# Context attention: transposes moved from TensorE to transposing DMA transfers, products of probabilities and values placed behind both projections of a round

## The reference, cut to what matters

```python
D_MODEL, H, KVH, HD, EPS = 512, 16, 4, 128, 1e-6
q = x @ Wq.T                          # 128 x 2048
k, v = cat(ctx, x) @ Wk.T, cat(ctx, x) @ Wv.T   # 256 x 512
q, k = rope(rms_norm(q)), rope(rms_norm(k))
p = softmax(q @ k.T / sqrt(HD))       # per head 128 x 256
x = layernorm(x + (p @ v) @ Wo.T)
```

## Time and profile before

| | us |
|---|---|
| median of 3 runs | 3000.09 (2999.1 to 3002.46) |
| profiled execution: its own time | 3004.53 |
| its span | 3002.7 |
| TensorE busy | 2727.9 (91%) |
| VectorE busy | 1958.4 (65%) |
| ScalarE busy | 1574.4 (52%) |
| GpSimd busy | 1204.2 (40%) |
| mean granted TensorE clock | 0.969 |

### The profile page before, as it was taken

How to read it: one execution, slowest core, us unless ns; L and a number is a source line. 1 busy time by engine, 2 the same in 40 slices (tenths; PEclk the granted TensorE clock), 3 DMA queues, 4 the chain that set the end, 5 groups by cost and what they waited for, 6 DMA issues and landing times. The chain is left out here.

```text
span 3002.7 us, 49266 instructions
## 1 busy us (share of the span) xinstructions
PE 2727.9 (91%) x17011; PEld 1595.3 (53%) x17276; DVE 1958.4 (65%) x3681; ACT 1574.4 (52%) x3629; POOL 1204.2 (40%) x1238
## 2 busy tenths in 40 slices
PE   6789896899999999959976998998889999999998
PEld 4677672555555555524434665666654444444443
DVE  5778896878787888767656788887463232322335
ACT  7999983655555555464417777676432221222121
POOL 3889885745454545224333111111142212222121
PEclk8999997999999999989997999999989999999999
DMA  4111103100000000040012000000021111111211
GB/s 161 40 54 48 43 33 120 43 5 8 4 7 4 7 4 4 1 168 1 1 50 74 19 19 18 14 16 19 12 90 65 45 50 63 63 63 32 65 32 67
DMA packets 50541, 122.53 MB, mean 41 GB/s; under 512 B 7042, under 2 KB 11522, under 8 KB 48163
## 3 DMA queue, kind: packets, MB, share of 16 engines
q1 hardware_dynamic: 50338, 120.00, 12.3%
HBM read 111.25 MB, written 4.52 MB: 39 GB/s over the span
## 5 line engine op out<-in xcount | busy, mean ns | idle before, releaser
L2060 POOL TENSOR_TENSOR s_state<-s_state,s_ct 128x512 f32<-128x512 f32 x256 | 326.8, 1302 | 82.0 <-DVE s_state L2235 79.6
L2235 DVE TENSOR_TENSOR_SCAN s_state<-s_decay,s_psd 128x512 f32<-128x512 f32 x256 | 301.8, 1208 | 68.3 <-PE s_psd L2380 34.7
L1044 DVE TENSOR_TENSOR m_prod<-m_bank,m_gated 128x512 f32<-128x512 f32 x88 | 60.8, 691 | 437.6 <-ACT m_gated L853 437.6
L779 POOL TENSOR_TENSOR m_aTl<-m_prod,m_aTh 128x512 bf16<-128x512 f32 x88 | 101.8, 1157 | 584.0 <-ACT m_aTh L855 584.0
L853 ACT ACTIVATE m_gated<-m_bank 128x512 f32<-128x512 f32 x88 | 52.5, 597 | 437.3 <-PE m_bank L1166 437.3
L1156 PE MATMUL m_bank<-m_xTl,m_wh 128*128 128x512 bf16 x704 | 267.8, 380 | 3.1 <-ACT m_wh L819 1.0
L1155 PE MATMUL m_bank<-m_xTh,m_wh 128*128 128x512 bf16 x671 | 255.5, 381 | 2.4 <-DVE m_prod L1044 2.4
L2380 PE MATMUL s_psd<-ident,s_v 128*128 128x128 f32 x1024 | 166.0, 287 | 41.8 <-DVE s_state L2235 21.1
L2136 ACT ACTIVATE s_decay<-s_dt,s_nega 128x508 f32<-128x508 f32 x256 | 181.6, 710 | 20.4 <-DVE s_state L2235 20.3
L2149 ACT ACTIVATE s_v<-s_uT,s_bT 128x512 f32<-128x512 f32 x256 | 182.1, 712 | 0.8 <-PE s_psd L2380 0.7
L2380 PEld LDWEIGHTS s_psd<-ident,s_v 128*128 128x128 f32 x1024 | 123.1, 147 | 88.6 <-ACT s_v L2149 47.1
(11 more groups left out here) (516 smaller groups left out, 8070.2 us busy)
## 6 DMA issues: line engine op xcount, KB each, us to landing
s_ct<-ssm_bc SPq DMA_DIRECT2D x64, 256.0 KB, 3.2
m_scale<-moe_scale SPq DMA_DIRECT2D x64, 256.0 KB, 3.2
m_stage<-in_moe_w_dram SPq DMA_DIRECT2D x16, 768.0 KB, 5.0
m_stage<-in_moe_w_dram SPq DMA_DIRECT2D x8, 864.0 KB, 7.8
X<-in_x_dram SPq DMA_DIRECT2D x4, 1024.0 KB, 12.2
a_cf<-in_ctxT_dram SPq DMA_DIRECT2D x16, 256.0 KB, 2.7
a_wstage<-in_xa_wq_dram SPq DMA_DIRECT2D x8, 512.0 KB, 3.6
a_wstage<-in_xa_wo_dram SPq DMA_DIRECT2D x8, 512.0 KB, 4.0
```

Source lines behind the costliest of these rows:

```text
L2060: pool.tensor_tensor(h, h, ct[t % 4][:, s * P:(s + 1) * P].unsqueeze(1).broadcast_to([P, KB, P]), ALU.mult).then_inc(weighted, 1)
L2235: dve.tensor_tensor_scan(state[i % RING][:, :], decay[t % 2][:, s, :, :].rearrange("p m t -> p (m t)"), ps_d[i % 2][:, :], 0.0, ALU.mult, ...
```

## The change: what it does, and its diff

The transposes of `rot` and of the probabilities leave TensorE. What is to be turned is first split in high and low part in SBUF (`rotp`, `pp`), and SyncE issues transposing DMA transfers, each of 128 partitions x 1024 bf16 values (eight blocks of 128 x 128, 256 KB): one for each chunk 0 to 5 (both parts in it), two for each round's probabilities (high, low). That is 14 transfers a turn. `ps_t` goes, and its two banks make `ps_p` four buffers deep. ScalarE's `prob_high` now scales and rounds in one instruction per head (L1588), VectorE's `prob_low` scales and subtracts in one per head (L1705), in the same round as the exponentials; `normalize` shrinks to the reciprocal (`totals`). `turned_high` reads SBUF, and `turned_low` moves to GpSimd. Products of probabilities and values (`values`, `attn_high`, `attn_low`) stand behind the second chunk. SyncE's program is written out turn by turn, with the last five `wo` loads between the transfers of turn 0. The LayerNorm's `r` shares memory with a weight staging buffer.

```diff
@@ SyncE
+            def turn_chunks(n, g, j):
+                if g == 0:
+                    return
+                for c in (2 * g - 2, 2 * g - 1):
+                    r = c % 2
+                    sp.wait_ge(t_low.sem, t_low.at(n, c + 1))
...
+                    sp.dma_start(out, rotp[r][:, :, :].rearrange("p a n -> p (a n)"), transpose=True).then_inc(t_done[r].sem, 16)
+
+            def turn_probs(s, g):
+                for a, ready, done in ((0, p_high, ph_done), (1, p_low, pl_done)):
+                    sp.wait_ge(ready.sem, ready.at(s, g + 1))
+                    if a == 0 and (g or late(s, 1)):
+                        sp.wait_ge(pv.sem, pv.at(s, g) if g else pv.at(s - 1))
+                    sp.dma_start(pT[:, a, :, :, :].rearrange("p k h q -> p (k h) q"),
+                                 pp[:, a, :, :, :].rearrange("p k h t -> p (k h t)"), transpose=True).then_inc(done.sem, 16)
+
+            def turn(s, p, start=None, last=False, last_x=False):
+                for g in range(4):
+                    if g == 0 and not last_x:
+                        context(s + 2)
+                    if not last:
+                        turn_chunks(s + 1, g, 1 - p)
+                    if start == 0 and g:
+                        wl.sync(sp, wlow, first_wo + 2 * g + 1, min(first_wo + 2 * g + 3, nchunks))
+                    turn_probs(s, g)
@@ GpSimd
+            def turned_low(n, c):
+                pool.wait_ge(t_high.sem, t_high.at(n, c + 1))
+                pool.tensor_tensor(rotp[c % 2][:, 1, :], rot[c % 2][:, :], rotp[c % 2][:, 0, :], ALU.subtract).then_inc(t_low.sem, 1)
...
+                    if g and not last:
+                        turned_low(s + 1, 2 * g - 2)
                     if not last_x:
...
+                    if g and not last:
+                        turned_low(s + 1, 2 * g - 1)
                     if not last:
                         front(s + 1, g, 1 - p)
@@ ScalarE
             def exponentials(s, g, p):
                 act.wait_ge(shifted.sem, shifted.at(s, g + 1))
                 if g or late(s, 1):
-                    act.wait_ge(p_turned.sem, p_turned.at(s, 2 * g) if g else p_turned.at(s - 1))
+                    act.wait_ge(p_low.sem, p_low.at(s, g) if g else p_low.at(s - 1))
...
+                for h in range(GH):
+                    e = act.activation(pp[:, 0, :, h, :], prob[:, h, :].rearrange("p (k t) -> p k t", k=2), ACT.Copy, scale=rtotal[:, h:h + 1])
@@ VectorE
                 if c >= 2 or late(n, 1):
-                    dve.wait_ge(turned.sem, turned.at(n, c - 1) if c >= 2 else turned.at(n - 1, 5 + c))
+                    dve.wait_ge(t_low.sem, t_low.at(n, c - 1) if c >= 2 else t_low.at(n - 1, 5 + c))
...
-                for h in range(GH):
-                    m = dve.tensor_scalar(prob[:, h, :], prob[:, h, :], rtotal[:, h:h + 1], None, ALU.mult)
...
+                for h in range(GH):
+                    m = dve.scalar_tensor_tensor(pp[:, 1, :, h, :], prob[:, h, :].rearrange("p (k t) -> p k t", k=2), rtotal[:, h:h + 1], pp[:, 0, :, h, :],
+                                                 ALU.mult, ALU.subtract)
@@ TensorE, a round
                     scores(s, g, p)
-                    if g:
-                        turn_probs(s, g - 1, t_low.at(s) if g == 1 or last else t_low.at(s + 1, 2 * g - 2))
...
                     if not last:
                         chunk(s + 1, 2 * g, 1 - p)
+                    if g == 0 and not last_x:
+                        turn_x(s + 2, p)
+                    if not last:
+                        chunk(s + 1, 2 * g + 1, 1 - p)
                     if g:
                         values(s, g - 1, p)
                     elif start != 0:
                         values(s - 1, 3, 1 - p)
-                    if g == 0 and not last_x:
-                        turn_x(s + 2, p)
-                    if not last:
-                        turn_chunks(s + 1, g, 1 - p)
-                        chunk(s + 1, 2 * g + 1, 1 - p)
```

More of the change, by code:

```diff
@@ L1252, in stage_xattn @@
         woh, wol = (fr.sb(f"a_wo{n}", [P, 16, D], BF16, st) for n in "hl")
-        ln = LayerNorm(fr, st, "a")
+        wstage = [fr.sb(f"a_wstage{j}", [P, 1024], F32, st)[:, :] for j in range(3)]
+        ln = LayerNorm(fr, st, "a", r=wstage[2][:, 0:D])
         xs = fr.sb("a_xs", [P, D], F32, st)
@@ L1330, in stage_xattn @@
         v_low = Count(fr, "a_vlow", 2)
-        turned = Count(fr, "a_turned", 6)
+        t_done = [Count(fr, f"a_tdone{r}", 48) for r in range(2)]
         t_high = Count(fr, "a_thigh", 6)
@@ L1376, in _ @@
             wl.sync(sp, wlow, 4, first_wo)
[L1377 to L1380, removed]
+            turn_chunks(0, 1, 0)
+            wl.sync(sp, wlow, first_wo, first_wo + 3)
+            turn_chunks(0, 2, 0)
+            turn_chunks(0, 3, 0)
+            turn(0, 0, start=0)
+            for s in range(1, SEQS - 2):
+                turn(s, s % 2)
+            turn(SEQS - 2, 0, last_x=True)
+            turn(SEQS - 1, 1, last=True, last_x=True)
         @block.gpsimd
@@ L1469, in _ @@
             c_low_part(1, 1)
-            for g in range(3):
+            for g in range(4):
+                if g:
+                    turned_low(0, 2 * g - 2)
+                    turned_low(0, 2 * g - 1)
                 if g == 1:
@@ L1551, in turn @@
                         chunk(s + 1, 2 * g, 1 - p)
+                    prob_high(s, g)
+                    if g and not last:
+                        turned_high(s + 1, 2 * g - 1)
+                    if g == 0 and not last_x:
+                        x_high_part(s + 2, p)
+                    if not last:
+                        chunk(s + 1, 2 * g + 1, 1 - p)
                     if g:
@@ L1693, in turn @@
                         chunk(s + 1, 2 * g, 1 - p)
+                    prob_low(s, g)
+                    if g == 2 and not last_x:
+                        bound(s + 2)
+                    if not last:
+                        chunk(s + 1, 2 * g + 1, 1 - p)
                     if g:
@@ L1697, in turn @@
                         attn_low(s - 1, 3)
-                    if not last:
-                        turned_low(s + 1, g, 1 - p)
-                    if g == 2 and not last_x:
-                        bound(s + 2)
-                    if not last:
-                        chunk(s + 1, 2 * g + 1, 1 - p)
                     if g == 1 and start is None:
@@ L1811, in values @@
                     cols = slice(g * HD, (g + 1) * HD)
[L1812 removed]
+                    mm = three(pe, ps_v[:, :], (vh[p][:, k, cols], vl[p][:, k, cols]), [pT[:, a, k, :, :].rearrange("p h q -> p (h q)") for a in range(2)], k == 0, k == 1)
                 mm.then_inc(pv.sem, 1)
@@ L1825, in turn @@
                     scores(s, g, p)
-                    if g:
-                        turn_probs(s, g - 1, t_low.at(s) if g == 1 or last else t_low.at(s + 1, 2 * g - 2))
-                    elif start != 0:
-                        turn_probs(s - 1, 3, t_low.at(s))
                     if not last:
                         chunk(s + 1, 2 * g, 1 - p)
+                    if g == 0 and not last_x:
+                        turn_x(s + 2, p)
+                    if not last:
+                        chunk(s + 1, 2 * g + 1, 1 - p)
                     if g:
```

163 lines of the change are left out of this document (64 added, 99 removed).

## The result

The changed kernel takes 3080.86 us (median of 4 runs, 3079.49 to 3085.03) where the kernel before took 3001.28 in the same comparison: 2.67% slower, ratio 1.0267 with an interval of 1.0249 to 1.0284. The forecast was 3020 with a range from 2972 to 3160: the direction and the range hold, the size does not (+80 instead of +20). The profiled execution has a span of 3077.7, 75.0 more than before.

What follows compares the result with a forecast made beforehand. TensorE's list bounds the kernel at 48.8 us a turn; with transfer waits the turn becomes 48.4. Twelve turns of -0.4 are -5, start +20, end +5: +20 on the median 3000.1 gives 3020, range 2972 to 3160.

Steps and rivals of the forecast that it cites:

- What TensorE saves: TensorE loses 56 transposes, 6.1 us a turn; its list with gaps falls from 48.8 to 42.7 us.
- the last part of the rivals: TensorE's granted clock may fall to 0.93, making its 42 us 45; worth up to 1 to 2 us a turn.
- The ring: VectorE, ScalarE and GpSimd, from one round's maxima to the next: without transfer waits, four rounds take 45.5 us a turn.
- I take 0.34, 1.36 for four: Price of VectorE's low part of the probabilities: 0.34 us per instruction, up to 0.42, 1.36 for a round's four.
- The transfers: Transposing transfers on SyncE's queue make TensorE wait 5.9 us a turn before the value products, giving a turn of 48.4.
- D: Queue time of one transposing transfer: 1.1 to 5.6 us, taken as 2.3; the prediction fails altogether below 1.8.
- rival 1: Transposing transfers are fast enough, so the other engines' cycle sets a turn of 45.5 us: 2975 us, chance 0.35.
- Rival 2: High and low parts at 0.46 and 0.42 lengthen the other engines' cycle: turn 48.2 us, time 3008 us, chance 0.12.
- its sign: Evidence for the longer cycle: VectorE's wait for ScalarE's high part would be long in every round; no size given.
- Start and end: First turns add 20 us, from transfers behind the `wo` loads and uncovered transfers; the last turn adds 5.
- SyncE's order: In turn 0 the probabilities' transfers stand behind `wo` loads waiting for GpSimd: 10 us, bounds 0 and 28.5.
- The values behind the second chunk: Placing the products of probabilities and values there gives TensorE 2.6 us of cover against waits for transfers.

Runs made afterwards that it cites:

- The two runs on form and place: Changed kernel with the probabilities' low part as TENSOR_TENSOR without the scaling, 3072.15 us; with its first operand read from the scores' PSUM tile, 3040.36 us.
- the two-round version: Changed kernel with a second probabilities buffer, their low part one round later, value products another round later, x's low part after the first chunk: 2974.01 us, ratio 0.9903.
- GpSimd's small instruction: Changed kernel with GpSimd's low part of the turned projections on 4 of 512 columns, the rest zeros: 3004.45 us, ratio 1.0001.

## Why the prediction was off by its size

- *What TensorE saves: right.* 642.8 to 549.4 us of busy time in a stretch that holds 12.4 turns instead of 13.4 is 44.4 a turn at a clock of 0.95, instead of 48.1; the forecast was 48.0 - 6.1 = 41.9 of work at full clock, 42.7 with the gaps. The kernel was no longer bound by TensorE, as predicted, and the clock fell as the last part of the rivals had it.
- *The ring: right in its order, wrong in one term, and this is the step that failed.* "I take 0.34, 1.36 for four" for the low part, with 0.42 as its worst. The four rounds were summed as 12.4, 13.0, 10.2, 9.3 and 0.6 for hand-offs, 45.5 (the 2.4 for ScalarE in round 0 is 2.24 by its own terms, which changes little); the maxima of the turn above start at 795.31, 810.07, 825.17, 837.05 and 847.91, so the rounds take 14.8, 15.1, 11.9 and 10.9, 52.6 in all, 7.1 more. The low parts in them take 3.46, 3.09, 2.56 and 2.93, which is 12.0 instead of 5.4. These 6.6 are the largest excess in the ring, but not simply 6.6 of the 7.1: the shifts, the normalization of X and the high parts are longer than priced as well, so the excesses together are more than 7.1 and some are hidden. What the runs give back a turn is 3.2 with the low part at 0.41 (and a new wait on TensorE), 5.0 with GpSimd's new work taken away. The forecast priced an instruction by the length of its work, 0.34. Alone it is 0.42, four in 1.67, the forecast's worst case; in this place, with both tensor operands in SBUF, GpSimd holds it up for another 0.35. With one in PSUM it is 0.41 in all company.
- *Where the row was misread.* The upper bound 0.42 came from a scaling that took 1.77 instead of 1.14 for four. I called that disturbed and took it for a cap; it was a sample of the mechanism. The change then removed a subtraction that took one operand from PSUM (`a_pst`) and put in one with two from SBUF, and gave GpSimd six instructions a turn more to collide with. The Trainium skill (SBUF — State Buffer, section Who interferes with whom) says just this: a VectorE instruction with two SBUF inputs contends with a GpSimd instruction that reads SBUF; one with at most one such input does not, unless it runs in a mode that uses both of VectorE's ports, which TENSOR_SCALAR can enter. The two runs on form and place agree (0.73 and 0.41 us each), and the run without the subtraction (TENSOR_SCALAR, 0.63) fits the exception, though no run here shows which mode it ran in. The prediction did not weigh that page.
- *The transfers: wrong, and without effect.* D was taken as 2.3. SyncE issues one in 1.28 and it lands 3.2 after, also when three stand one behind the other, so they land about 1.3 us apart: D is below the 1.8 that the prediction named as its own point of failure. TensorE's waits for them are there (43.4 us in 500, 4.6 a turn, where the forecast had 5.9), but they lie in slack. By rival 1's words the turn should then have been 45.5; what made it 52.7 was the longer ring. The forecast of 48.4 rested on a wait that does not count.
- *Rival 2 was the nearest* (the ring is longer), with a worst case of 0.22 a pair where 0.53 was measured (0.42 and 0.11). It got 0.12. It had the place and not the reason: it knew nothing of GpSimd, and its sign, a long wait of VectorE for the high part in every round, is not there (8.9 us in 500, in round 3 alone). That the time lies inside the stated range is luck: the range's upper part was made of slow transfers.
- *Start and end: near in size, the reason open.* 17.4 instead of 20, 9.0 instead of 5. Taking GpSimd's low part away makes the start 13 shorter (626.16 instead of 639.52), but moving it to VectorE only 2 (637.47) and the low part from PSUM 7 (632.87). So the collision is part of it, and GpSimd's low part on the way to the transfers may be another; they were not told apart. SyncE's order, to which I gave 10, was worth nothing in the run that changed it. That run had the two-round version as its base, so for the changed kernel itself it is an inference.
- *The values behind the second chunk* were credited with 2.6 us of cover; they cost 1.2 a turn.

Open: how the 5.0 us that GpSimd's small instruction gives back divides between the holding and the earlier release of `rot`, which of the excesses in the ring are hidden, and why the earlier values gain.

## What to carry to other kernels

When a change moves an instruction's operand from PSUM to SBUF, or work onto GpSimd, lay VectorE's and GpSimd's rows side by side and count the VectorE instructions that would run beside GpSimd with two SBUF operands, and those of the form TENSOR_SCALAR that read SBUF: both were held up here, by up to 1 us each. A duration that varies between equal instructions is a mechanism to be found, not a bound. And a long wait on an engine proves nothing about the turn until the thing waited for is made cheap; copying instead of transposing took most of TensorE's wait away and left the time as it was.

## What the runs showed of the hardware that I had not expected

- An instruction of four columns (`a_shift`, 0.16 us alone) takes up to 1.05 beside GpSimd. Halving the 256 columns of a low part saves 0.13 us of 0.76, as much as it saves alone; the 0.35 us of holding stays.
- The holding goes both ways: GpSimd's addition took 2.08 instead of 1.26 beside VectorE's subtraction, which kept its 0.68 there.
- A transposing transfer of 128 x 1024 bf16 from SBUF to SBUF lands 3.2 us after its issue, a plain one of the same bytes 2.3 to 2.9; three issued in a row land about 1.3 us apart. Transposing raises the DMA share of the steady stretch from 0.23 to 0.40 and costs this kernel's turn nothing.
